# Softmax passes of a graph network: the slots of PE's, DVE's and ACT's hand-overs, the order of the picks, and the distance from a step to its scaled row

## The reference, cut to what matters

```
e = leaky_relu(es[src] + ed[dst])            # L1, four heads; e == 0 becomes -1000
m = segment_max(e, dst)
alpha = exp(e - m[dst]) / segment_sum(exp(e - m[dst]), dst)
out = segment_sum(alpha * z[src], dst)       # rows of 256 columns
...
out = out_before + self loop                 # L2a (four heads), L2b (one head, 64 columns)
...
scores = sum(q[dst] * k[src]) / 16 + edge_weight * we + be        # L3, one head, softmax as above
```

## Time and profile before

| | |
|---|---|
| median of 3 runs | 3149.26 us (3144.26 to 3154.49) |
| span of the profiled execution | 3626.7 us |
| its own time around the span | not given |
| granted TensorE clock, mean over the span | 0.711 |
| busy: PE, PEld, DVE, ACT, POOL | 2379.2, 1641.7, 1987.0, 1393.1, 2230.6 us |
| gathers | 392 in L0, 416 in each of the other four passes |

### The profile page before, as it was taken

How to read it: one execution, slowest core, us unless ns; L and a number is a source line. 1 busy time by engine, 2 the same in 40 slices (tenths; PEclk the granted TensorE clock), 3 DMA queues, 4 the chain that set the end, 5 groups by cost and what they waited for, 6 DMA issues and landing times.

```text
span 3626.7 us, 45558 instructions
## 1 busy us (share of the span) xinstructions
PE 2379.2 (66%) x9551; PEld 1641.7 (45%) x9551; DVE 1987.0 (55%) x7379; ACT 1393.1 (38%) x3670; POOL 2230.6 (62%) x2460
## 2 busy tenths in 40 slices
PE   5655556838777774667777624554556588888888
PEld 2323334724444442344444424444454356555567
DVE  4554446536666673566666813333345366666677
ACT  2444544413333343333333513333343244444444
POOL 5666663566676657666766356666644366666636
PEclk7677677955666677666666755555555789999999
DMA  6656654234444423344444122222212255555411
GB/s 198 176 173 169 172 173 135 63 107 113 114 115 115 114 68 101 108 114 114 116 115 113 26 44 45 47 47 45 47 36 74 74 154 154 155 155 154 148 53 49
DMA packets 247934, 389.14 MB, mean 107 GB/s; under 512 B 58944, under 2 KB 161366, under 8 KB 247673
## 3 DMA queue, kind: packets, MB, share of 16 engines
q0 software_dynamic: 92032, 230.64, 24.6%
q1 hardware_dynamic: 155641, 155.59, 14.0%
HBM read 331.11 MB, written 54.91 MB: 106 GB/s over the span
## 4 chain that ended last, share of the span: by engine, by line
PE 39%; issue 21%; DVE 15%; another core or an unknown queue 14%; POOL 4%; ACT 3%; DVEq 2%; DMA 1%; SPq 0%; POOLq 0%; ACTq 0%
PE PS L1798 20%; PE PS L1719 6%; PE PS L1690 4%; DVE ACC L1323 3%; PE PS L1852 3%; POOL work L690 2%; DVE ACC L1090 1%; DVE work L1294 1%; PE PS L1776 1%; POOL rstd L579 1%; DVEq L376 1%; PE PS L1835 1%; PE PS L1748 1%; PE PS L1769 1%
## 5 line engine op out<-in xcount | busy, mean ns | idle before, releaser
L690 POOL DMA_INDIRECT work<-t_z,srcK x1248 | 1228.2, 984 | 610.8 <-issue 302.5
L1798 PE MATMUL PS<-work,M 128*128 128x260 f32 (+3 forms) x3328 | 1303.0, 512 | 447.6 <-issue 229.0
L1798 PEld LDWEIGHTS PS<-work,M 128*128 128x128 f32 x3328 | 757.4, 270 | 672.1 <-issue 480.2
L1323 DVE TENSOR_TENSOR ACC<-ACC,PS 128x260 f32 (+3 forms) x1614 | 588.7, 365 | 212.7 <-PE PS L1798 117.6
L2026 ACT ACTIVATE M<-iota,dloc 128x128 f32<-128x128 f32 x1248 | 396.9, 389 | 665.3 <-PE PS L1798 308.4
L690 POOL DMA_INDIRECT work<-t_x,srcK x416 | 394.0, 947 | 269.5 <-PE PS L1798 142.2
L690 POOL DMA_INDIRECT work<-in_x,srcTile x392 | 374.8, 956 | 212.2 <-issue 103.7
L1690 PE MATMUL PS<-work,M 128*128 x832 | 313.0, 519 | 240.8 <-issue 120.0
L1690 PEld LDWEIGHTS PS<-work,M 128*128 128x128 f32 x832 | 187.5, 250 | 361.5 <-issue 338.6
L1294 DVE TENSOR_TENSOR work<-work 128x256 f32<-128x256 f32 x800 | 329.1, 412 | 22.4 <-issue 14.2
L1719 PE MATMUL PS<-Y,w 128*128 x832 | 282.3, 425 | 72.2 <-issue 34.8
(11 more groups left out here) (266 smaller groups left out, 2928.9 us busy)
## 6 DMA issues: line engine op xcount, KB each, us to landing
work<-t_dhot SPq DMA_DIRECT2D x416, 128.0 KB
t_hot<-M SPq DMA_DIRECT2D x104, 256.0 KB
M<-t_hot SPq DMA_DIRECT2D x104, 256.0 KB
work<-t_z,srcK POOLq DMA_INDIRECT x1248
t_dhot<-work SPq DMA_DIRECT2D x104, 128.0 KB
work<-t_edge SPq DMA_DIRECT2D x104, 64.0 KB
work<-t_x,srcK POOLq DMA_INDIRECT x416
t_z<-Y SPq DMA_DIRECT2D x50, 130.0 KB, 2.0
```

The source lines that it names most:

```text
L690: pool.indirect_dma_start(out=slots[:, j, 0:width], out_offset=None, in_=table[:, :], in_offset=bass.IndirectOffsetOnAxis(ap=sources[:, k: ...
L1323: ins = vec.tensor_tensor(sums, sums, PS[k % SUMS[stage]][:, 0:cols], ALU.add)
L1798: mm(PS[k % n][:, 0:cols], M[:, k % (4 * G), :], slots_of[:, k % RING[stage], 0:cols], start=True, stop=True)\
```

## The change

The chain's slots are spread: DVE takes up what PE has turned or folded two slots later, where it was the same or the next slot. PE follows DVE by one slot as before. The chain of a group now runs from slot 2 to slot 20, so that the last five slots of one group (peaks, exponentials, alphas) fall into slots 0 to 4 of the next; the loops of DVE, PE and ACT call them with g - 1 and q + 16. ACT's exponential and its copy of the alphas, one function before, are two (`make_exps`, `put_alphas`); in L3 they have slots 18 and 19, in the GAT passes one follows the other directly. SOFAR goes from 31 to 36, and with it scaling, sum, add and fade of every step move five slots back, and each pass has five more slots. PE's picks for the next group are made two a slot in slots 6 to 13 of this one, in place of one a slot. The number of instructions stays the same. The diff, cut to the lines that move something (names and lines of the kernel before are put behind them):

```
-SOFAR = 31
+SOFAR = 36
...
                 def inside(g, q, early):                      # DVE
-                    if q == 5 and not early:                  L1206, scan before
+                    if q == 7 and early:
-                    elif q == 6 and early:                    L1210, scan behind
+                    elif q == 7:
-                    elif q == 6:                              L1214, ends
+                    elif q == 8 and early:
...
                 def across(g, q, early):                      # DVE
-                    if q == 8 and early:                      L1228, chain forward
+                    if q == 11 and early:
-                    elif q == 8:                              L1234, chain back
+                    elif q == 11:
-                    elif q == 9 and early:                    L1240, fan
+                    elif q == 12 and early:
-                    elif q == 9 and g:                        L1249, climb
+                    elif q == 12 and g:
-                    elif q == 10 and early and g and heads > 1:
+                    elif q == 13 and early and g and heads > 1:
...
                 def peaks(g, q, early):                       # DVE
-                    if q == 11 and not early:                 L1260, starts
+                    if q == 16 and early:
-                    elif q == 12 and early:                   L1265, scan upto
+                    elif q == 16:
-                    elif q == 12:                             L1269, scan peak
+                    elif q == 17 and early:
-                    elif q == 13 and early:                   L1275, fall
+                    elif q == 17:
-                    elif q == 15 and early and topped:        L1280, tops
+                    elif q == 20 and early and topped:
...
                     for early in (True, False):               # DVE's loop
+                        if 0 <= g - 1 < NG:
+                            peaks(g - 1, q + GS, early)
                         if 0 <= g < NG:
                             logits(g, q, early)
                             inside(g, q, early)
                             across(g, q, early)
-                            peaks(g, q, early)
...
-                    elif q == 7:                              # PE's turns, L1759: ends
+                    elif q == 9:
-                    elif q == 11:                             L1766: fan, climbs
+                    elif q == 14:
-                    elif q == 14:                             L1779: exponentials
+                    elif q == 18:
...
                     g, q = divmod(t - GS, GS)                 # PE's loop
+                    if 0 <= g - 1 < NG:
+                        turns(g - 1, q + GS)
                     if 0 <= g < NG:
                         turns(g, q)
...
-                        for k in (() if q == 2 else (t - 3, t - 2) if q == 3 else (t - 2,)):
-                            if 0 <= k < STEPS:
-                                pick(k)
+                        if 6 <= q < 6 + GS // 2 and g + 1 < NG:
+                            for i in range(2):
+                                pick(GS * (g + 1) + 2 * (q - 6) + i)
...
+            def make_exps(stage, g):                          # ACT
+
+                R = GS * HEADS_OF[stage]
+                act.wait_ge(fall_made.sem, fall_made.at(stage, g + 1))
+                sc.activation(expd[0:R, :], fall[0:R, :], ACT.Exp).then_inc(exps_made.sem, 1)
+
             def put_alphas(stage, g):
-                act.wait_ge(fall_made.sem, fall_made.at(stage, g + 1))
-                sc.activation(expd[0:R, :], fall[0:R, :], ACT.Exp).then_inc(exps_made.sem, 1)
                 act.wait_ge(exps_turned.sem, exps_turned.at(stage, g + 1))
...
+                    make_exps(stage, g)                       # gat_edges of ACT
                     put_alphas(stage, g)
...
-                    if q == 12 and g:                         # row_edges of ACT
+                    if q == 15 and g:
                         fade_open(stage, g)
-                    elif q == 14:
+                    elif q == 18:
+                        make_exps(stage, g)
+                    elif q == 19:
                         put_alphas(stage, g)
...
+                    if 0 <= g - 1 < NG:
+                        chain(g - 1, q + GS)
                     if 0 <= g < NG:
                         chain(g, q)
```

More of the change, by code:

```diff
@@ L1205, in inside @@
                     x = PS[5][0:R, 0:P]
-                    if q == 5 and not early:
+                    if q == 7 and early:
                         dve.wait_ge(logits_turned.sem, logits_turned.at(stage, g + 1))
@@ L1209, in inside @@
                             .then_inc(inside_made.sem, 1)
-                    elif q == 6 and early:
+                    elif q == 7:
                         dve.wait_ge(inside_made.sem, inside_made.at(stage, 2 * g + 1))
@@ L1227, in across @@
                     back = chain_back[0:heads, :]
-                    if q == 8 and early:
+                    if q == 11 and early:
                         dve.wait_ge(ends_turned.sem, ends_turned.at(stage, g + 1))
@@ L1239, in across @@
                                                ALU.add, ALU.max).then_inc(chain_made.sem, 1)
-                    elif q == 9 and early:
+                    elif q == 12 and early:
                         dve.wait_ge(chain_made.sem, chain_made.at(stage, 2 * g + 2))
@@ L1248, in across @@
                             ALU.mult).then_inc(fan_made.sem, 1)
-                    elif q == 9 and g:
+                    elif q == 12 and g:
                         vec.tensor_scalar(climb[0:heads, :], last, back[:, 0:1], 0.0, ALU.subtract, ALU.min)\
                             .then_inc(climb_taken.sem, 1)
-                    elif q == 10 and early and g and heads > 1:
+                    elif q == 13 and early and g and heads > 1:
                         dve.wait_ge(climb_taken.sem, climb_taken.at(stage, 2 * g - 1))
@@ L1259, in peaks @@
                     x = PS[5][0:R, 0:P]
-                    if q == 11 and not early:
+                    if q == 16 and early:
                         dve.wait_ge(fan_turned.sem, fan_turned.at(stage, g + 1))
@@ L1264, in peaks @@
                         vec.tensor_copy(starts[0:R, :], small[0:R, 64:66]).then_inc(starts_put.sem, 1)
-                    elif q == 12 and early:
+                    elif q == 16:
                         dve.wait_ge(starts_put.sem, starts_put.at(stage, g + 1))
@@ L1268, in peaks @@
                             .then_inc(peaks_made.sem, 1)
-                    elif q == 12:
+                    elif q == 17 and early:
                         dve.wait_ge(peaks_made.sem, peaks_made.at(stage, 2 * g + 1))
@@ L1274, in peaks @@
                                                ALU.add, ALU.max).then_inc(peaks_made.sem, 1)
-                    elif q == 13 and early:
+                    elif q == 17:
                         dve.wait_ge(peaks_made.sem, peaks_made.at(stage, 2 * g + 2))
@@ L1279, in peaks @@
                         vec.tensor_tensor(fall[0:R, :], x, peak[0:R, :], ALU.subtract).then_inc(fall_made.sem, 1)
-                    elif q == 15 and early and topped:
+                    elif q == 20 and early and topped:
                         slot = GS * g % RING[stage]
@@ L1765, in turns @@
                         last.then_inc(ends_turned.sem, 1)
-                    elif q == 11:
+                    elif q == 14:
                         pe.wait_ge(fan_made.sem, fan_made.at(stage, g + 1))
```

3 lines of the change are left out of this document (removed).

## The result

The changed kernel takes 3180.93 us (median of 4 runs, 3179.14 to 3184.28); the kernel before, beside it, 3149.73 us (4 runs, 3144.26 to 3154.49). The ratio is 1.0103, 95% interval 1.0091 to 1.0114: 1.0% slower, +31.2 us.

The account below looks back on a forecast made before the run. The prediction took POOL's gathers, about 1.25 us a step, to bound the passes. Terms of +17.0 (tails), +3.8 (L3's start) and -3.7 (hops) gave +17.1 us on 3149.3, so 3166 us (+0.54%), overall range 3078 to 3185.

Parts of the forecast that it names:

- What bounds the kernel: In timed runs POOL's gathers, about 1.25 us a step, bound the passes and cover the softmax hand-overs.
- far down: Sign of being right: PE's waits for scaled rows (L1294, L1297), 117.7 us in the profile, would mostly go.
- The faster rival: Others than POOL bound the passes, so half of PE's 184.8 us of waits returns: 3078 us; chance 0.30.
- The 48 us left over: Profiled span less 430 us of gather delays gives 3197 us against 3149 measured; put to cheaper gathers or delays between passes.
- Part 1, the hops: Wider PE-to-DVE hops: worth nothing under the gathers' floor, at most 7.4 us at the ends of GAT passes; -3.7 us taken.
- slot 7 also holds two scans: Crowded DVE slot 7, about 3.2 us of work: gathers cover it, zero; else 1 to 2 us a group, up to 150.
- Part 2, the picks: Picks two a step in slots 6 to 13: zero; up to 156 us if the loads' cover went.
- Part 3, the distance: Five more slots a pass: +17.0 us after the last gathers, bounds 0 to 29.2, and +3.8 us at L3's first sum.
- The start of L3: With the ring of 48 full, five more slots at 0.75 us each delay the first free slot by +3.8 us.
- Short ring: With POOL's lead 11 rows, not 16, its waits for sums grow: 3223 us, much slower; chance 0.07.
- main case: Gathers bound the passes and tails get longer: slower, own range 3150 to 3180 us; chance 0.50.
- Same: Rival: looser hops give back 13 us in L3, offsetting the tails: 3149 to 3158 us, say 3154; chance 0.13.

Follow-up runs that it names:

- second profile of before: Kernel before, unchanged, profiled again for a trace without the long "remote" waits: span 3136.7 us, own time 3138.61 us.
- the earlier trace: First profile of the kernel before, unchanged, which the prediction read: span 3626.7 us against a timed median of 3149.26 us.
- the later rounds: Kernel before, unchanged, timed again on three later occasions beside the follow-up runs: medians 3142.5, 3140.8 and 3143.0 us.
- e10_l2b_one_source: Kernel before plus an extra 128x256 multiplication of one SBUF tensor by a constant at each of 376 steps of L2b: 3152.09 us, ratio 1.0028.

## Why the prediction was right, and where it was not

**What bounds the kernel: right.** Gathers at 1.25 us a step are the floor. In the second profile of before POOL's gap between two gathers is never over 0.32 us in L1, L2a, L2b and L3, whatever is named as its releaser. PE's 245.9 us of hand-over waits in the earlier trace rows were no reserve. For scaled rows (L1294 and L1297) it waits 455.6 us in the second profile of before (231.4 + 224.2) and 457.5 after (257.7 + 199.8), where "far down" was expected. The faster rival had its price from these rows, and they are the floor itself, seen from PE. The granted clock was 0.758 in the second profile and 0.751 after, and 0.771 in the slowest kernel of all (hops and distance), so the time does not follow it.

**The 48 us left over: the second of two guesses.** The prediction took 430 us off the profiled span and had 48 us too many left, which it gave to cheaper gathers ("0.024 us for each") or to "the delays between the passes". A gather costs 0.946 us at the median in both profiles. From the first to the last gather the five passes are indeed 432 us shorter in the second profile, but that this equals the 430 is luck: L1 and L2a lost 61 and 69 us in place of 84 each, since their long gathers stayed, and L3 lost 142 in place of 91, since its stand of 50.9 us went too. What was left over lies behind the gathers: the four tails are together 48 us shorter. So the reckoning of the floor had no term for long gathers, whose excess in L1 and L2a is 37.6 us in the second profile (23.1 + 14.5). The sign was in the earlier trace rows: minimum and median agree in all passes, but the longest is 1.4 to 1.65 us in L0, L1 and L2a and 1.10 in L2b. With the median as the price of a gather I did not ask what makes some of them long.

**Part 1, the hops: the step that failed.** "Under the gathers' floor it is worth nothing, because POOL issues no sooner" took the floor for a constant. It is not: what DVE runs at a gather's start decides how long it takes, and the new slot 7 puts L1208, L1294 and L1212 side by side, in L2a right at a gather's start. Measured: +23.9 us in L2a's gathers in place of -3.7. "What becomes late next is the group's last gathered row" was right (L1178's 555.5 us). For "slot 7 also holds two scans ... gathers cover it" I had priced PE's next need, and not POOL. The prediction cited one page on the clock; the page that bore on it is another. The Trainium skill, SBUF — State Buffer, "Who interferes with whom", says that a DVE instruction with two SBUF inputs contends with a GpSimd instruction that reads SBUF. The trace agrees: the gather reads its column of indices (srcK) there, and one that meets such an operation at its start is up to 0.4 us longer. I had not weighed it. That it is this read that is held up no run shows.

**Part 2, the picks: right** (1.0002 alone). In company with the hops they seem to give 6 us back; their place shifts DVE's logits and so the phases, but which of them was not tried.

**Part 3, the distance: right in kind and nearly in size.** Here a tail is again counted from the last gather's start to the last sum. After the last landing 33 sums are left in L1, L2a and L2b and 41 in L3, in place of 28 to 30 and 33. The tails went from 41.5, 43.9, 35.0 and 27.1 us to 44.8, 47.3, 35.9 and 32.2, so +12.7 against +17.0 - 3.7 = +13.3. The distance alone gave 47.0, 48.5, 37.6 and 30.3, so +15.9 for the +17.0; the hops took 5.1 off the three GAT tails, for the 3.7 of credit, and put 1.9 on L3's. The start of L3 was priced at +3.8: the first spread to the first sum went from 22.7 to 27.5 us, and POOL, which did not stand at all there in the second profile, now does:

```profile
2542.58 0.95 POOL L690 DMA_INDIRECT work<-t_x,srcK  x1 [0.30 <-issue]
2547.74 0.95 POOL L690 DMA_INDIRECT work<-t_x,srcK  x1 [4.21 <-PE PS L1799]
```

L3's gathers span 5.1 us more. The 50.9 us of the earlier trace rows belonged to that one execution. These two terms together, 12.7 + 5.1 = 17.8, stand beside the predicted 17.1; the distance alone measured +23, of which 6.1 is L2a's excess (20.6 against 14.5 us).

**The sum.** +17.8 from the predicted terms, +23.9 from the missed one, +4.1 of scatter in L0 and elsewhere make the 45.8 us between the two profiles. The medians of that comparison differ by 31.2 only; against the 3142 us of the later rounds it would be 38 to 40. The forecast's 3166 us was low because the hops were taken as covered by the gathers, and the cover itself gave way. The direction came from the right term; of the measured +31 the prediction had 17, and 3180.93 us lies just outside the main case's own range of 3150 to 3180. It is inside the overall range only by the 5 us by which that one reaches further, and no mechanism stands behind these.

**The rivals.** Short ring: POOL is held up by sums in L3's start alone, 4.2 us. Same: L3 gave nothing back. The chance of 0.30 on the faster one rested on rows of a disturbed execution.

## What to carry to other kernels

An engine that issues indirect gathers is not alone with its clock: when it is the bound, look at its longest instructions, not only at the median, and at what DVE does in their first tenths of a microsecond. Operations with two tensors in SBUF belong behind that point, or take one operand from PSUM or as a scalar. And where gathers are the floor, slack inside a group is worth nothing and distance costs: five slots more lengthened the four tails by 15.9 us in all, and the wider hops only made DVE wait longer for the last row. The way back is not simply the reverse: seven slots fewer, with the hops packed, took 5.1 us off three tails, and most of the gain of 19 us came from less excess of the long gathers; in L3 the packed chain lost 27 us. So try a shorter chain pass by pass, and look at the gathers in each trace.

## What the runs showed of the hardware that I had not expected

- An indirect gather of 128 rows costs POOL 0.946 us and 0.30 us before the next; a memset of 0.12 us fits into these 0.30 without cost.
- A VectorE operation with two SBUF tensors that runs at a gather's start lengthens it, mostly by 0.1 to 0.4 us (0.68 the most). Where no such operation ran under the gather, one of the same length with a PSUM source at its start (42 gathers), or a shorter one with a single SBUF source (30 gathers), lengthened none by over 0.051 us.
- The single-source 128x256 operation took 0.285 us at the median. In 35 of its 376 cases it took 0.39 to 0.51; all of these began 0.6 to 0.9 us after a gather's start, and what holds them is not shown. The Trainium skill, SBUF — State Buffer, "Who interferes with whom", lists `tensor_scalar` among the operations that can contend with GpSimd, when their operands meet certain conditions. In run e10_l2b_one_source it lengthened none of those 30 gathers by over 0.05 us; whether this one ran in such a mode no row here tells.
- The same program can spend hundreds of us more in waits that the profile puts down to "remote" and to PE (3626.7 against 3136.7 us). A profile whose span is far above the median is to be taken again before its waits are priced.
